# Six of 32 loop sums as three bf16 matmuls on split values, in a fused two-layer graph kernel

## What is computed

```python
h = x @ W.T
g = h @ Wg.T
vals = (h + b) * sigmoid(g + bg)             # one relation: loop; the other 39 find no edges in these inputs
out = relu(adj_t_is_1 @ vals)                # "loop sum"
x = layernorm(x + out)
y = sum_r (adj == r) @ x @ weight[r] + bias  # "messages", then "message weights"
x = layernorm(x + y)
```

## Time and profile before

| | |
|---|---|
| median of 3 runs | 158.95 us (158.8 to 159.37) |
| profiled execution, its own time | 159.41 us |
| its span, first to last instruction | 157.7 us |
| PE busy | 148.8 us (94%) |
| DVE busy | 124.1 us (79%) |
| ACT busy | 122.8 us (78%) |
| POOL busy | 125.7 us (80%) |
| mean granted TensorE clock | 0.987 |

### The profile page before, as it was taken

How to read it: one execution, slowest core, us unless ns; L and a number is a source line. 1 busy time by engine, 2 the same in 40 slices (tenths; PEclk the granted TensorE clock), 3 DMA queues, 4 the chain that set the end, 5 groups by cost and what they waited for, 6 DMA issues and landing times.

```text
span 157.7 us, 3520 instructions
## 1 busy us (share of the span) xinstructions
PE 148.8 (94%) x1040; PEld 136.7 (87%) x1040; DVE 124.1 (79%) x325; ACT 122.8 (78%) x255; POOL 125.7 (80%) x195
## 2 busy tenths in 40 slices
PE   7999999999999999999999999999999999999910
PEld 3688999999999999999999999999999999999800
DVE  1359988888988888887988888887888878989980
ACT  3357876979797997979797997979797997769850
POOL 0606698797979799797979799797979799797970
PEclk9999999999999999999999999999999999999995
DMA  4899999989797988979797989989693929211053
GB/s 126 292 405 394 370 389 404 390 265 389 198 382 230 331 303 258 354 241 398 177 392 209 356 290 286 340 237 373 192 393 130 381 92 303 86 69 69 4 201 138
DMA packets 19606, 42.73 MB, mean 271 GB/s; under 512 B 2177, under 2 KB 3073, under 8 KB 19585
## 3 DMA queue, kind: packets, MB, share of 16 engines
q1 hardware_dynamic: 14544, 25.76, 48.6%
q0 software_dynamic: 4752, 16.52, 30.3%
q10 hardware_dynamic: 288, 0.20, 0.4%
HBM read 34.08 MB, written 8.39 MB: 269 GB/s over the span
## 4 chain that ended last, share of the span: by engine, by line
POOL 65%; PE 15%; issue 13%; DVE 1%; POOLq 1%; ACT 0%; DVEq 0%
POOL rstd L339 31%; POOL x L353 26%; PE hg_ps L423 7%; POOL adj_sb L326 4%; POOL adjt_sb L333 3%; PE loop_ps L439 2%; PE msg_ps L458 2%; PE msg_ps L413 1%; PE y_ps L497 1%; PE hg_ps L407 1%; POOL rstd L363 1%; POOLq L59 1%; DVE s_sb L808 0%; ACT gate L607 0%; POOLq L234 0%
## 5 line engine op out<-in xcount | busy, mean ns | idle before, releaser
L339 POOL TENSOR_TENSOR rstd<-var,power 128x8 f32<-128x8 f32 (+1 forms) x36 | 53.8, 1496 | 18.5 <-DVE var L787 18.4
L423 PE MATMUL hg_ps<-w_all,xt_sb 128*128 128x256 f32 x256 | 65.7, 382 | 0.0
L353 POOL TENSOR_SCALAR x<-s_sb,mean_neg,rstd 128x128 f32<-128x128 f32 x120 | 52.2, 448 | 3.4
L423 PEld LDWEIGHTS hg_ps<-w_all,xt_sb 128*128 128x128 f32 x256 | 44.6, 193 | 4.1 <-issue 0.3
L626 ACT ACTIVATE out_sb<-z_sb,rstd 128x128 f32<-128x128 f32 x120 | 38.1, 390 | 0.4 <-POOL rstd L339 0.4
L800 DVE TENSOR_TENSOR vals<-hg_ps,gate 128x512 f32<-128x512 f32 x32 | 22.1, 690 | 19.3 <-ACT gate L607 19.3
L439 PEld LDWEIGHTS loop_ps<-vals,adj_sb 128*128 128x128 f32 x256 | 33.3, 191 | 1.9 <-issue 0.2
L598 ACT ACTIVATE hg_ps<-gate_b 128x1024 f32<-128x1024 f32 (+1 forms) x32 | 31.8, 998 | 3.2 <-DVE vals L800 2.6
L458 PEld LDWEIGHTS msg_ps<-adjt_sb,x 128*128 128x128 f32 x248 | 31.4, 191 | 3.1 <-issue 1.5
L439 PE MATMUL loop_ps<-vals,adj_sb 128*128 128x128 f32 x256 | 33.8, 275 | 0.1
L458 PE MATMUL msg_ps<-adjt_sb,x 128*128 128x128 f32 x248 | 33.2, 277 | 0.0
(11 more groups left out here) (64 smaller groups left out, 48.2 us busy)
## 6 DMA issues: line engine op xcount, KB each, us to landing
xt_sb<-x_t_dram SPq DMA_DIRECT2D x32, 256.0 KB, 4.9
x_sb<-x_dram SPq DMA_DIRECT2D x32, 256.0 KB, 4.2
out<-out_sb SPq DMA_DIRECT2D x31, 256.0 KB, 4.7
adj_sb<-adj_dram POOLq DMA_DIRECT2D x15, 512.0 KB, 5.2
adjt_sb<-adj_t_dram POOLq DMA_DIRECT2D x15, 512.0 KB, 6.5
adjt_sb<-adj_t_dram POOLq DMA_DIRECT2D x2, 256.0 KB, 6.7
first_edges<-adj_dram SPq DMA_DIRECT2D x1, 256.0 KB, 4.2
adj_sb<-adj_dram POOLq DMA_DIRECT2D x1, 256.0 KB, 6.3
```

What stands on the lines that cost most here:

```text
L339: nc.gpsimd.tensor_tensor(rstd[:, c % RSTD_RING, first:end, :].rearrange("p l b -> p (l b)"), var[:, c % 2, first:end, :].rearrange("p l b ...
L353: done = nc.gpsimd.tensor_scalar(x1[:, q % X1_RING, batch(b)], s_sb[:, q % S_RING, batch(b)], mean_neg[:, c % 2, b:b + 1], rstd[:, c % RST ...
L423: last = nc.tensor.matmul(hg_ps[:, q % 2, b, :], xt_sb[:, q % XT_RING, batch(b)], w_gate, start=False, stop=True, skip_group_check=True)
```

## The change

The loop sums of groups 7, 11, 15, 19, 23 and 27 (`SPLIT`) are made in another way. A 32-bit float of `vals` is cut into three 16-bit floats (bf16): its own upper half, read in place with a step of two; the upper half of what is left (`below` = vals minus its upper half); and the rest (`lowest`, stored as bf16). The adjacency's floats 0.0 and 1.0 are read by their upper halves too. The four matmuls of 32-bit floats become twelve of bf16, accumulated by threes in the same bank. DVE gets two instructions per split group, after `first_sum(t-1)` and before `first_stats(t-1)`, the second behind a wait for the first; `loop_sum(q)` of a split group waits for `split_done` as well. The other 26 loop sums stay as they were.

```diff
@@
+SPLIT = tuple(range(7, GROUPS - 4, 4))
@@
+        below = sb("below", [P, W], F32)
+        lowest = sb("lowest", [P, W], BF16)
@@
+        def upper_half(tile):
+            return tile.bitcast(BF16).rearrange("p (n two) -> p n two", two=2)[:, :, 1]
+
@@
                     pe.wait_ge(vals_done, q + 1)
+                    if q in SPLIT:
+                        pe.wait_ge(split_done, SPLIT.index(q) + 1)
 
                     await_count(pe, s_done, q)
                     for b in range(GB):
-                        last = nc.tensor.matmul(loop_ps[:, batch(b)], adj_sb[:, spot, batch(b)],
-                                                vals[:, q % 2, batch(b)], start=True, stop=True)
+                        if q in SPLIT:
+                            edges = upper_half(adj_sb[:, spot, batch(b)])
+                            nc.tensor.matmul(loop_ps[:, batch(b)], edges, upper_half(vals[:, q % 2, batch(b)]),
+                                             start=True, stop=False)
+                            nc.tensor.matmul(loop_ps[:, batch(b)], edges, upper_half(below[:, batch(b)]),
+                                             start=False, stop=False)
+                            last = nc.tensor.matmul(loop_ps[:, batch(b)], edges, lowest[:, batch(b)],
+                                                    start=False, stop=True)
+                        else:
+                            last = nc.tensor.matmul(loop_ps[:, batch(b)], adj_sb[:, spot, batch(b)],
+                                                    vals[:, q % 2, batch(b)], start=True, stop=True)
                     last.then_inc(loop_done, 1)
@@
+            def split(q):
+                await_count(dve, loop_done, q - 1)
+                dve.wait_ge(vals_done, q + 1)
+                tt(below[:, :], vals[:, q % 2, :], upper_half(vals[:, q % 2, :]), ALU.subtract).then_inc(below_done, 1)
+                dve.wait_ge(below_done, SPLIT.index(q) + 1)
+                tt(lowest[:, :], below[:, :], upper_half(below[:, :]), ALU.subtract).then_inc(split_done, 1)
+
@@
             for t in range(3, GROUPS - 2):
                 values(t)
                 first_sum(t - LOOP_LAG)
+                if t in SPLIT:
+                    split(t)
                 if t == 3:
                     first_norm1(1)
                 first_stats(t - LOOP_LAG)
```

More of the change, by code:

```diff
@@ L165, in build @@
         vals_done = sem("vals_done")
+        below_done = sem("below_done")
+        split_done = sem("split_done")
         loop_done = sem("loop_done")
```

## The result

The changed kernel took 166.16 us in the median of 4 runs (166.09 to 167.03), against 158.88 for the kernel before: the ratio is 1.0451, with a 95% interval from 1.0418 to 1.0484. The forecast was 166.0 us. The profiled execution took 166.18 us, its span is 164.4 us, 6.7 more than before.

A forecast was written before the change was run, and what follows sets the result against it. PE is full and x1 arrives only just in time; late `var` adds 5 x 1.2 + 0.98 = 7.0 us to the profiled 159.41, making 166.4, and the median 0.46 lower gives 166.0 us. Range 162.6 to 169.1 us.

The forecast's parts named there:

- What bounds the kernel: PE is busy 94% of the span, yet x1 arrives just in time: `messages` has 0 to 0.25 us to spare.
- The delay of `var`: On DVE, two added instructions of 0.69 us each before the statistics make `var` 1.23 us late in split steps.
- How far it travels: Through POOL's x1 to PE: `messages(10)` 0.98 us later, `messages(11)` 1.2; five splits at 1.2, the last at 0.98.
- PE's part at nothing: Split loop sums on PE, 0.25 us less or 0.39 more each, cost nothing because PE waits for x1 anyway.
- rival 3: PE's bf16 passes are dear, 191 ns each: twelve take 2.29 us, 167.4 us in all; chance 0.04.
- The port: DVE's `below` may meet POOL's fourth x1 instruction: if POOL loses, `messages(9)` moves 0.65 us, sum unchanged; if DVE, +2.9.
- the first rival: DVE loses the shared SBUF port to POOL's x1 instruction: + 9.9, that is 168.9 us; chance 0.18.
- The signs: Changed profile: `var` some 1.2 us later, POOL's wait near 2.0, six PE holes of about 1 us, PE about 90% busy.
- 2: The two DVE instructions are cheap, 0.43 us each, so `var` is delayed 0.71: 162.8 us; chance 0.08.
- 4: Faster: DVE's spare time hides the delay of `var` and PE keeps its gain of 1.5 us: 157.4 us; chance 0.05.
- 5: Nothing: the delay stays hidden in DVE's spare time, but x1's chain denies PE its gain: about 159 us; chance 0.03.

The follow-up runs named there:

- The 24 cheaper loop sums: Kernel before, with the loop sums of groups 4 to 27 made by bf16 matmuls of `vals`' upper half only, nothing added on DVE: 158.67 us, ratio 0.9947.
- DVE's half: Changed kernel with the two DVE instructions and the wait for them, but all loop sums made by matmuls of 32-bit floats: 166.64 us, ratio 1.0472.
- PE's half: Kernel before, with six loop sums made by twelve bf16 matmuls reading only `vals`' upper half, nothing added on DVE: 159.27 us, ratio 1.0004.
- the kernel with PSUM operands: Changed kernel, but both new DVE instructions take their first operand from PSUM, so each has one SBUF input: 166.18 us, ratio 1.0431.
- the two statistics instructions: Kernel before, plus two unused 256-element statistics instructions on DVE in six steps: 162.07 us after the first sum, 159.19 us before `vals`.
- after the variances: Changed kernel with the two DVE instructions moved from before the statistics to behind the variances: 161.43 us, ratio 1.0134.

## Why the prediction was right

**What bounds the kernel.** Right: PE's work and x1's chain lie within a few hundredths of each other. The 24 cheaper loop sums that brought 0.8 us, and six that brought nothing, show that x1 sets the pace as soon as PE needs less.

**The delay of `var`.** Forecast 1.23, measured 1.24. `below` took 0.685 and `lowest` 0.756 on average, where 0.69 was taken for both; the next instruction started 0.66 behind `lowest`'s start (55.51 to 56.17).

**How far it travels.** Forecast 0.98 in `messages(10)` and 1.2 with the step behind it. Measured 0.41 + 0.58 = 0.99, then 1.18, and 0.07 more that I had not seen. The first split took 1.34, and the last, put at 0.98, took 1.07. Six such differences are the 0.4 us by which 7.0 was short of 7.4 in the steps that the splits touch; the shorter head of this execution hides it in the span. That the median agrees with 166.0 to 0.2 us is in part luck: the medians differ by 7.3, and the forecast had 7.0.

**PE's part at nothing.** Right, and shown by DVE's half alone. The estimate for a bf16 pass was 0.053 to 0.107, with 0.053 as the fair value; it is 0.057, so the gain is 0.21 a loop sum and not 0.25. Reading with a step of two cost nothing that shows: in PE's half, where all twelve passes read both operands so, they take 0.69, and 0.68 with `lowest` read without a step (rival 3 needed 0.17 a pass).

**The port.** The engines met as the first rival said they might, but POOL lost: its fourth x1 instruction took 0.96 to 0.98 in all six splits (0.52 more), and `below` kept its 0.68 (0.70 in the first). The prediction had put 0.65 in `messages(9)` for this case, where 0.41 was measured, and said that it would lie inside the delay that comes anyway; the kernel with PSUM operands shows just that. On the Trainium skill's rule (SBUF — State Buffer, sections "Who interferes with whom" and "SBUF: two separate sides") the runs agree in one part: with two SBUF inputs the instructions collide (0.96 to 0.98 for POOL's fourth), and with one they do not (0.45 to 0.46). The other part, that whichever starts first gets the port for its whole instruction, does not fit the records: in five of the splits POOL's instruction begins 0.05 to 0.07 before `below` (54.74, 54.79), in the first 0.05 after it (35.81, 35.76), and in all six it is POOL that waits. What it loses, 0.52, is less than the 0.68 of `below`. The profile's spans on POOL are rough, so the true order of the starts stays open.

**The signs.** The two DVE instructions and the delay of `var` came as listed. POOL's wait for `var` is 1.58 and not near 2.0, and the hole in front of `messages(10)` is 0.56 and not about 1 us, because the collision had already made `messages(9)` 0.41 late; with one SBUF input for each instruction they are 2.03 and 0.99. PE's busy share fell to 92%, not to 90%.

**The rivals.** 2 (cheap DVE instructions) falls by their durations. 4 and 5 rested on DVE's idle time; the two statistics instructions show that it is free before `vals`, where a split of this step's `vals` can't be made, and not behind the first sum.

## What to carry to other kernels

Idle time on an engine is not a reserve as such: ask which instruction it lies in front of, and put added work there (it cost nothing that shows here), or behind the last result that another engine waits for (2.4 us in place of 7.3 here). Where two engines take turns at setting the pace, work taken from one of them brings nothing while the other's chain stays as long; look for the distance between a result's end and its user's start before pricing the saving. And a split that makes matmuls cheaper has to be paid for on the engine that makes the parts: here 1.24 us on the chain for 0.21 us of PE work.

## What was not expected of the hardware

- Three matmuls of bf16 parts are together cheaper than the one of 32-bit floats that they replace: 0.68 us against 0.89 for four graphs, and 0.69 when every pass reads both operands with a step of two.
- When DVE's difference of two SBUF tiles (0.68) met POOL's x1 instruction, POOL lost some 0.52 in each of the six splits; when `below` and `lowest` both met POOL's power, 0.37 (2.01 against 1.64). DVE lost some 0.05, in `lowest` (0.74 against 0.69 after the variances), except in the first split, where `lowest` took 0.82 and `below` 0.70.
